# A decoder layer on one core: a second buffer and another order for the transposed probabilities of the cross attention

## The chip, the cores and the metric

The kernel runs on one core of a Trainium2 chip. The metric is the device time of one launch in microseconds; the lower the better. Five engines work beside each other: TensorE (PE), VectorE (DVE), ScalarE (ACT), GpSimd (POOL) and the DMA-issuing SyncE (SP). TensorE reads SBUF and writes PSUM, which has eight banks of 128 partitions by 512 fp32 values.

## What is computed

One pre-norm decoder layer on x of (8, 100, 512) with a context of (8, 361, 256), all fp32. Cut to its frame:

```python
x = x + attn(layernorm(x), ...)             # rope, 16 query heads on 4 key heads
x = x + xattn(layernorm(x), ctx_1024, ...)  # the part that the change touches
x = x + ffn(layernorm(x), ...)              # shared expert, and top 4 of 60 experts

# xattn, 16 heads of 32, 345 context rows and 16 more with weights of their own ("dca")
q = ln(x @ Wq + bq); k = ln(y_main @ Wk + bk); v = y_main @ Wv + bv
k_dca = ln(y_dca @ Wk_dca + ...); v_dca = ...
ctx = softmax(q @ k.T * SCALE) @ v + softmax(q @ k_dca.T * SCALE) @ v_dca
out = ctx @ Wo + bo
```

## The kernel before

**The whole.** One program with five hand-written instruction streams, one per engine, that meet at semaphores. After a preamble (weights, the dca keys) comes a loop over four pairs of batch rows; pair i holds batches 2i and 2i+1, called j = 0 and 1. Each turn does the self attention, the projections of the context, the cross attention, the output projection, the third layer norm and the router's gate. After the loop come the shared expert, the sorting of tokens to experts, the 60 experts in 20 rounds, and the gathering of the results. The change is in the cross attention of the loop alone.

**Steps.** The cross attention of a pair has 32 heads (two batches of 16), in 8 groups of four, `FOURS`. The TensorE stream walks `STEPS` = 10 steps, t = 0 to 9 (`for t in range(STEPS)`, line 1016 on). In step t it issues, in this order:

- `four_scores(t)` (L913), the scores of group t: four products of 32 rows by 345 columns, head r into bank r. It waits until ScalarE has emptied all four banks of the group before.
- `four_values(t - 2)` (L935): twelve products of 115 rows and 32 columns with the transposed probabilities of group t - 2. In steps 2 and 6, where a batch begins, a product with a tile of zeros (L930) first clears the whole bank (6 or 7), so that the others only add to it.
- `four_transposes(t - 1, c)` for c = 0 and 1 (L922): the probabilities of group t - 1, cut into three parts c of 115 rows; four transposes each.
- the work of `STEP_HOOKS`, that is other work hung on a step: a transpose of the queries in 3, dca scores in 4 (L883), dca transpose and the spread of the sums in 5 (L891, L947), the output projection of batch 0 in 6 (L787), dca transpose in 8. In step 5 `context_end(0)` (L900) follows behind everything.
- `four_transposes(t - 1, 2)`.

The parts c go to banks 4 and 5 by turns, so part 2 takes the bank of part 0 and can only begin when part 0 has been copied away.

**The other engines.** VectorE takes for each head the negated maximum (`four_max`, L1666), and copies the transposed parts from PSUM to `xpT` (`four_T`, L1670). Its stream also holds the layer norm of the next pair, cut into small linked pieces that `few(n)` drops between the others, n at a time. Its order in step t is

```python
four_max(t, 0); four_max(t, 1); few(1)
four_max(t, 2)
four_T(t - 1, 0)
four_max(t, 3)
few(2); four_T(t - 1, 1)
few(2); four_T(t - 1, 2)
few(2)
```

with `context_T(0)` behind the second maximum of step 6, and in step 7 `residual("xo", 0)` and the start of the third layer norm behind the fourth maximum. ScalarE takes the exponentials with their sums (`four_exp`, L1276), one for each head, into SBUF, and copies only the very last part 1 (L1325). There is one buffer `xpT` for the three parts of a group. `q_T(1)` (L1234) on ScalarE stands behind the exponentials of step 3; the scores of step 4 wait for it.

## Time and profile before

| | |
|---|---|
| median of 3 runs | 1371.33 us (1367.48 to 1371.35) |
| profiled execution, its own time | 1366.12 us |
| its span | 1364.3 us |
| busy shares of the span | PE 85%, PE weight load 45%, DVE 36%, POOL 29%, ACT 18% |
| mean granted clock of TensorE | 0.882 |
| chain that ended last | PE 48%, POOL 18%, DMA 11%, issue 11%, DVE 6% |

A busy time is what an engine's instructions take, without register, branch, semaphore and DMA-issuing ones. The profile marks for each stretch the granted clock of TensorE (PEclk): 1.00 is 2.4 GHz, 0.50 is 1.2 GHz, and a number between them means that part of the stretch had the one and part the other. Ends of matmuls are modelled, so the starts are what to compare. fp32 matmuls show as two records each, transposes as one.

### The profile page before, as it was taken

To read this page: it belongs to the slowest core of one execution; us is meant where nothing else is said; L and a number is where in the kernel's file an instruction comes from. 1 tells how busy PE (TensorE), PEld (TensorE's weight loads), DVE (VectorE), ACT (ScalarE), POOL (GpSimd) and SP (SyncE) were. 2 spreads that over 40 slices of the span, in tenths; PEclk is the share of its full clock that TensorE was granted. 3 is DMA by queue.
4 is the path that set the end of the run, shared out by engine and by line. 5 is a ranking of instruction groups with operands and counts; after the bars stand their busy time and mean duration, and the time that the engine had idled before them with its cause. 6 is when DMAs were issued, how large, how long until landed. Compare 5 with 4: busy or idle time off the path is not lost.

```text
span 1364.3 us, 18670 instructions
## 1 busy us (share of the span) xinstructions
PE 1165.7 (85%) x5358; PEld 617.7 (45%) x5358; DVE 493.3 (36%) x1360; ACT 251.2 (18%) x788; POOL 396.6 (29%) x917
## 2 busy tenths in 40 slices
PE   2988989888899899898879989999898989989920
PEld 0444564446544465444646544335444444444400
DVE  7342645337553474526644601002121212111224
ACT  0141321323231241413312000001010101111100
POOL 4686206852088403874000170000000000000045
PEclk8999679986899877997679998999898989999965
DMA  9997000000100001002027285008999999999835
GB/s 317 341 392 273 1 20 32 22 0 1 33 19 22 0 2 51 1 1 83 1 79 197 70 268 217 0 0 318 386 386 381 387 389 392 387 383 390 323 107 149
DMA packets 76438, 232.71 MB, mean 171 GB/s; under 512 B 11346, under 2 KB 13750, under 8 KB 68670
## 3 DMA queue, kind: packets, MB, share of 16 engines
q1 hardware_dynamic: 58686, 197.55, 40.0%
q10 hardware_dynamic: 11520, 20.98, 4.3%
q0 software_dynamic: 6144, 13.13, 3.3%
q8 instruction: 41, 0.67, 0.2%
q14 instruction: 47, 0.39, 0.1%
HBM read 178.40 MB, written 53.22 MB: 170 GB/s over the span
## 4 chain that ended last, share of the span: by engine, by line
PE 48%; POOL 18%; DMA 11%; issue 11%; DVE 6%; SPq 2%; POOLq 2%; ACT 1%; DVEq 0%; ACTq 0%
PE ps L1048 9%; DMA arena<-in_w 7%; PE ps L1125 6%; PE ps L1098 6%; PE ps L1121 5%; PE ps L787 4%; POOL arena L663 4%; PE ps L922 3%; PE ps L1156 3%; PE ps L1152 3%; DMA arena<-ys_d,slot_u 2%; PE ps L913 2%; POOL arena L660 2%; PE ps L935 2%; POOL arena L685 2%
## 5 line engine op out<-in xcount | busy, mean ns | idle before, releaser
L787 PE MATMUL ps<-arena 128*100 128x512 f32 (+3 forms) x576 | 233.8, 562 | 5.6 <-ACT arena L1223 3.7
L734 POOL DMA_INDIRECT arena<-ys_d,slot_u x32 | 34.6, 1082 | 503.1 <-issue 498.4
L787 PEld LDWEIGHTS ps<-arena 128*100 128x100 f32 (+1 forms) x576 | 95.1, 188 | 121.7 <-issue 111.5
L1125 PE MATMUL ps<-arena 128*64 128x352 f32 x640 | 115.4, 520 | 29.0 <-issue 17.0
L1048 PE MATMUL ps<-arena 128*128 128x400 f32 x352 | 126.4, 519 | 15.2 <-issue 8.3
L869 PE MATMUL ps<-arena 128*100 128x512 f32 x256 | 114.5, 592 | 0.0
L1874 DVE COPY arena<-ps 128x512 f32<-128x512 f32 x40 | 27.7, 692 | 229.0 <-PE ps L1113 229.0
L1048 PEld LDWEIGHTS ps<-arena 128*128 128x128 f32 x352 | 69.2, 198 | 71.0 <-issue 22.0
L1121 PE MATMUL ps<-arena 128*128 128x352 f32 x320 | 98.0, 459 | 1.2 <-DVE arena L1874 1.2
L1125 PEld LDWEIGHTS ps<-arena 128*64 128x64 f32 x640 | 53.5, 154 | 83.2 <-issue 63.4
L1276 ACT ACTIVATE arena<-ps,arena 100x345 f32<-100x345 f32 x128 | 69.1, 546 | 119.2 <-DVE arena L1666 118.7
L922 PE MATMUL ps<-ident,arena 100*115 100x100 f32 x384 | 75.2, 354 | 11.1 <-DVE arena L1670 11.1
L1098 PE MATMUL ps<-arena 128*100 128x512 f32 x176 | 75.8, 592 | 0.7 <-DVE arena L1853 0.7
L1368 ACT ACTIVATE arena<-ps 128x352 f32<-128x352 f32 x40 | 18.6, 465 | 312.9 <-PE ps L1121 168.8
L922 PEld LDWEIGHTS ps<-ident,arena 100*115 100x115 f32 x384 | 64.5, 254 | 24.1 <-DVE arena L1670 12.7
L1121 PEld LDWEIGHTS ps<-arena 128*128 128x128 f32 x320 | 59.2, 190 | 31.0 <-DVE arena L1868 1.4
L869 PEld LDWEIGHTS ps<-arena 128*100 128x100 f32 x256 | 42.0, 167 | 59.7 <-issue 57.3
L1666 DVE TENSOR_REDUCE arena<-ps 100x1 f32<-100x345 f32 x128 | 60.8, 508 | 20.3 <-PE ps L913 19.2
L1670 DVE COPY arena<-ps 115x400 f32<-115x400 f32 x92 | 52.6, 572 | 41.6 <-PE ps L922 41.5
L723 POOL DMA_INDIRECT xs_d<-arena,slot_u x32 | 31.9, 998 | 104.6 <-DVE ov_i L1841 95.1
L663 POOL TENSOR_TENSOR arena<-arena 115x256 f32<-115x256 f32 (+7 forms) x128 | 57.7, 451 | 10.0
L1156 PE MATMUL ps<-arena 128*64 128x512 f32 (+1 forms) x240 | 56.0, 601 | 0.7 <-DVE arena L1890 0.7
(209 smaller groups left out, 1456.6 us busy)
## 6 DMA issues: line engine op xcount, KB each, us to landing
arena<-in_w SPq DMA_DIRECT2D x60, 1408.0 KB, 12.6
arena<-in_w SPq DMA_DIRECT2D x60, 512.0 KB, 13.6
xs_d<-zero SPq DMA_DIRECT2D x5, 3328.0 KB, 26.0
arena<-in_w SPq DMA_DIRECT2D x60, 192.0 KB, 14.3
arena<-xs_d ACTq DMA_DIRECT2D x40, 256.0 KB, 8.0
ys_d<-arena ACTq DMA_DIRECT2D x40, 256.0 KB, 7.6
ys_d<-zero SPq DMA_DIRECT2D x2, 3328.0 KB, 24.8
arena<-in_se_up SPq DMA_DIRECT2D x11, 512.0 KB, 3.4
```

The lines of the kernel that those rows point to most:

```text
L663: then(nc.gpsimd.tensor_tensor(s3[:, :, 0:w], s3[:, :, 0:w], s3[:, :, w:2 * w], ALU.add))
L787: last = nc.tensor.matmul(ps[0:m, k, 0:cols[1] - cols[0]], lhs(c), w[:, c, cols[0]:cols[1]], start=(c == 0), stop=(c == n_c - 1))
L869: last = nc.tensor.matmul(ps[0:S, j, :], cT[c % 2][:, g, :], w_out[:, c * G + g, :], start=(c == 0 and g == 0), stop=(c == KV - 1 and g == ...
L922: last = nc.tensor.transpose(ps[0:LC, k, r * S:(r + 1) * S], xp[(4 * t + r) % NP_][0:S, c * LC:(c + 1) * LC], ident[0:S, 0:S])
L1048: last = nc.tensor.matmul(ps[:, (u % 3) * 2 + gu, 0:400].rearrange("p (a b) -> p a b", a=4), se_w[m % 3][:, c, gu * P:(gu + 1) * P], tok, ...
L1098: last = nc.tensor.matmul(ps[0:S, b % 4, :], hT_all[:, m, b * S:(b + 1) * S], w_down[:, m, :], start=(m == 0), stop=(m == MC - 1))
L1121: last = nc.tensor.matmul(ps[:, 1 + gu, 0:I], xsT[0][:, c, :], w13_s[s][0][:, c, at:at + I], start=(c == 0), stop=(c == DC - 1))
L1125: last = nc.tensor.matmul(ps[half * HALF:(half + 1) * HALF, 3 + gu, 0:I], xsT[1][:, c, half * HALF:(half + 1) * HALF], w13_s[s][1 + half][ ...
L1156: last = nc.tensor.matmul(ps[half * HALF:(half + 1) * HALF, 7, :], hT[1][0:w, n, half * HALF:(half + 1) * HALF], w2_s[s][1 + half][0:w, n, :],
L1276: nc.scalar.activation(xp[(4 * t + r) % NP_][0:S, :], ps[0:S, k, 0:LM], ACT.Exp, bias=xnm[0:S, j, h:h + 1], scale=1.0, accum_out=xsum[0:S, ...
L1666: nc.vector.tensor_reduce(xnm[0:S, j, h:h + 1], ps[0:S, k, 0:LM], AX, ALU.max, negate=True).then_inc(xmax_ready.sem, 1)
L1670: nc.vector.tensor_copy(xpT[0:LC, c, :], ps[0:LC, k, 0:4 * S]).then_inc(free[k].sem, 1)
```

## The change

Four edits go together:

1. `xpT` becomes two buffers, used by turns (t % 2). The second lies in SBUF space that held keys and values of the self attention (`behind_kr`).
2. In the TensorE stream the transposes of parts 0 and 1 stand straight behind the scores, and `four_values(t - 2)` behind them. The table of bank fills is changed to match. The zero product that begins a batch now reads all 128 rows of the zero tile instead of one; its columns are the same.
3. In the VectorE stream the four maxima of a step stand together, with `few(1)` after the second; the copies of parts 0 and 2 follow, each behind a `few(2)`. In step 6 `context_T(0)` goes behind the fourth maximum. In step 7 the residual and the start of the norm now stand ahead of both copies.
4. The copy of part 1 goes to ScalarE, behind the four exponentials of the step (in step 3 ahead of `q_T(1)`).

```diff
@@ attention_fills
         if t < FOURS:
             out += [(("xs", t, r), r) for r in range(4)]
+        parts = [(("xpT", t - 1, c), 4 + (t * LN_ + c) % 2) for c in range(LN_)] if 1 <= t <= FOURS else []
+        out += parts[:2]
         if t in (2, 6):
             out.append((("ctx", (t - 2) // 4), 6 + (t - 2) // 4))
-        parts = [(("xpT", t - 1, c), 4 + (t * LN_ + c) % 2) for c in range(LN_)] if 1 <= t <= FOURS else []
-        out += parts[:2] + [(key, 7 if t < 6 else 6) for key in STEP_HOOKS.get(t, [])] + parts[2:]
+        out += [(key, 7 if t < 6 else 6) for key in STEP_HOOKS.get(t, [])] + parts[2:]
@@ buffers
-        xpT = pT.rearrange("p a b c -> p (a b c)")[:, 0:LN_ * 4 * S].rearrange("p (a b) -> p a b", a=LN_)
+        behind_kr = arena[:, kr_at:kr_at + LN_ * 4 * S]
+        assert LN_ * 4 * S <= 3 * D
+        xpT = [v.rearrange("p (a b) -> p a b", a=LN_) for v in (pT.rearrange("p a b c -> p (a b c)")[:, 0:LN_ * 4 * S], behind_kr)]
@@ TensorE
-                        nc.tensor.matmul(ps[:, 6 + j, 0:DC * S], zero[0:1, 0:P], zero[0:1, 0:DC * S], start=True, stop=False)
+                        nc.tensor.matmul(ps[:, 6 + j, 0:DC * S], zero[:, 0:P], zero[:, 0:DC * S], start=True, stop=False)
...
-                    if t >= 2:
-                        four_values(t - 2)
                     if 1 <= t <= FOURS:
                         four_transposes(t - 1, 0)
                         four_transposes(t - 1, 1)
+                    if t >= 2:
+                        four_values(t - 2)
@@ ScalarE
+                def four_T(t):
+                    k = filled("xpT", t, 1)
+                    nc.scalar.activation(xpT[t % 2][0:LC, 1, :], ps[0:LC, k, 0:4 * S], ACT.Copy).then_inc(free[k].sem, 1)
...
+                    if t:
+                        four_T(t - 1)
                     if t == 3:
                         q_T(1)
@@ VectorE
                     four_max(t, 0)
                     four_max(t, 1)
+                    few(1 if t else 0)
+                    four_max(t, 2)
+                    four_max(t, 3)
                     if t == 6:
                         context_T(0)
-                    few(1 if t else 0)
-                    four_max(t, 2)
-                    if t:
-                        four_T(t - 1, 0)
-                    four_max(t, 3)
                     if t == 7:
                         residual("xo", 0)
                         run(pieces)
                         dve.wait_ge(x1_ready, i * 2 + 4)
                         pieces = norm_x(0)
                     if t:
-                        for c in (1, 2):
+                        for c in (0, 2):
                             few(2)
                             four_T(t - 1, c)
```

Two places of the order. Lines of the kernel before are 5 to 10 less than those of the same statement after. First VectorE, the second half of step 3, before; L1666 is a maximum, L1670 a copy of a transposed part, the rest are pieces of the norm:

```order
L1666 TENSOR_REDUCE arena<-ps 100x1
L403 REGISTER_ALU
L1670 COPY arena<-ps 115x400
L1666 TENSOR_REDUCE arena<-ps 100x1
L1434 REGISTER_ALU
L1477 TENSOR_SCALAR arena<-arena 100x1
L1434 REGISTER_ALU
L1453 TENSOR_SCALAR arena<-arena 100x1
L1454 TENSOR_SCALAR arena<-arena 100x1
L403 REGISTER_ALU
L1670 COPY arena<-ps 115x400
```

The same place in the change, where L1676 is the maximum and L1680 the copy:

```order
L1676 TENSOR_REDUCE arena<-ps 100x1 x2
L1444 REGISTER_ALU
L1487 TENSOR_SCALAR arena<-arena 100x1
L1444 REGISTER_ALU
L1463 TENSOR_SCALAR arena<-arena 100x1
L1464 TENSOR_SCALAR arena<-arena 100x1
L408 REGISTER_ALU
L1680 COPY arena<-ps 115x400
```

The first copy of the step, that of part 0, has moved from between the maxima to behind both of them and behind two pieces of the norm; one of three copies is gone.

Second TensorE, step 4, before (L913 scores, L935 values, L922 transposes, L883 dca scores):

```order
L913 MATMUL ps<-arena 100x345 x4
L935 MATMUL ps<-arena 32x100 x4
L409 REGISTER_ALU
...
L935 MATMUL ps<-arena 32x100 x4
L922 MATMUL ps<-ident,arena 115x100 x8
L880 REGISTER_ALU
L883 MATMUL ps<-arena 100x64 x4
L765 REGISTER_ALU
L922 MATMUL ps<-ident,arena 115x100 x4
```

And in the change (L918 scores, L927 transposes, L940 values, L888 dca scores):

```order
L918 MATMUL ps<-arena 100x345 x4
L770 REGISTER_ALU
L927 MATMUL ps<-ident,arena 115x100 x4
L770 REGISTER_ALU
L927 MATMUL ps<-ident,arena 115x100 x4
L940 MATMUL ps<-arena 32x100 x12
L885 REGISTER_ALU
L888 MATMUL ps<-arena 100x64 x4
L770 REGISTER_ALU
L927 MATMUL ps<-ident,arena 115x100 x4
```

The eight transposes have moved ahead of the twelve values, which now stand in one run; the last four transposes stay at the end of the step.

## Rows read from the trace of the kernel before

**Rows 1.** The granted clock of TensorE in 40 slices of the span.

```profile
PEclk8999679986899877997679998999898989999965
```

**Rows 2.** Busy times by stretch, pair 0, steps 2 to 7; the columns stand first.

```profile
core 0: us, PE busy (x) PEld busy (x) DVE busy (x) ACT busy (x) POOL busy (x), PEclk, DMA share, GB/s
148.55:155.01 6.46, 6.37 (x46) 4.26 (x47) 4.24 (x15) 2.34 (x8) 5.00 (x15) 0.53 0.02 4
155.01:161.40 6.39, 5.89 (x49) 4.39 (x49) 6.05 (x21) 2.92 (x9) 0.00 (x0) 0.50 0.00 1
161.40:167.88 6.48, 6.48 (x53) 5.02 (x53) 3.73 (x14) 2.34 (x8) 0.00 (x0) 0.50 0.01 3
167.88:176.43 8.55, 8.12 (x60) 6.36 (x59) 5.63 (x14) 3.07 (x10) 0.77 (x1) 0.50 0.00 0
176.43:186.42 9.99, 9.99 (x55) 5.57 (x54) 3.33 (x7) 2.65 (x9) 0.00 (x0) 0.67 0.01 2
186.42:196.58 10.16, 7.60 (x88) 5.82 (x87) 8.15 (x25) 3.07 (x10) 0.72 (x1) 0.84 0.01 2
```

**Rows 3.** The same of pair 1, steps 5 and 6, and of pair 2, step 3.

```profile
332.83:339.42 6.59, 6.16 (x60) 4.59 (x59) 5.64 (x14) 3.07 (x10) 0.79 (x1) 0.71 0.00 0
339.42:346.30 6.88, 6.88 (x55) 3.76 (x55) 3.33 (x7) 2.64 (x9) 0.00 (x0) 1.00 0.01 2
...
480.92:487.06 6.14, 4.60 (x49) 3.00 (x49) 5.93 (x22) 2.92 (x9) 0.00 (x0) 0.78 0.01 4
```

**Rows 4.** The same, cross attention of each pair, scores of step 0 to the gate.

```profile
136.02:201.02 65.00, 57.99 (x416) 38.81 (x417) 39.96 (x119) 22.77 (x74) 10.01 (x25) 0.64 0.01 2
301.33:360.58 59.25, 52.20 (x416) 34.66 (x417) 39.60 (x119) 22.78 (x74) 10.02 (x25) 0.70 0.01 2
462.88:521.19 58.31, 50.52 (x416) 33.31 (x417) 39.46 (x119) 22.77 (x74) 10.03 (x25) 0.73 0.01 2
624.24:689.34 65.10, 58.06 (x416) 38.78 (x417) 39.95 (x119) 22.78 (x74) 10.02 (x25) 0.63 0.05 19
```

**Rows 5.** Timeline of TensorE, pair 0, steps 1 and 2: start, length, work, [wait].

```profile
147.36 0.65 PE L922 MATMUL ps<-ident,arena 100*115 100x100 f32 x4 [2.21 <-DVE arena L1670]
148.55 1.19 PE L913 MATMUL ps<-arena 32*100 32x345 f32 x8 [0.54 <-ACT arena L1276]
149.44 1.54 PE L930 MATMUL ps<-zero 1*128 1x400 f32 x2
152.06 2.86 PE L922 MATMUL ps<-ident,arena 100*115 100x100 f32 x12
```

**Rows 6.** Timeline of VectorE, pair 0, step 1.

```profile
146.74 0.56 DVE L1670 COPY arena<-ps 115x400 f32<-115x400 f32 x1
```

**Rows 7.** Timeline of TensorE, pair 0, step 4.

```profile
161.40 1.49 PE L913 MATMUL ps<-arena 32*100 32x345 f32 x8 [0.49 <-ACT arena L1234]
162.81 1.23 PE L935 MATMUL ps<-arena 115*32 115x100 f32 x24
163.97 1.87 PE L922 MATMUL ps<-ident,arena 100*115 100x100 f32 x8
166.91 1.04 PE L922 MATMUL ps<-ident,arena 100*115 100x100 f32 x4
```

**Rows 8.** Timeline of VectorE, pair 0, step 4.

```profile
162.87 0.94 DVE L1666 TENSOR_REDUCE arena<-ps 100x1 f32<-100x345 f32 x2 [1.10 <-PE ps L913]
```

**Rows 9.** Timeline of TensorE, pair 0, steps 7 and 8.

```profile
186.42 0.84 PE L913 MATMUL ps<-arena 32*100 32x345 f32 x8
189.45 0.65 PE L922 MATMUL ps<-ident,arena 100*115 100x100 f32 x4 [0.56 <-DVE arena L1670]
191.99 0.38 PE L935 MATMUL ps<-arena 115*32 115x100 f32 x8 [1.59 <-DVE arena L1670]
```

**Rows 10.** Groups by line and form, pair 0, steps 1 to 6.

```profile
L1276 ACT ACTIVATE arena<-ps,arena 100x345 f32<-100x345 f32 x24 | 13.0, 545 | 26.0 <-DVE arena L1666 25.8
L1670 DVE COPY arena<-ps 115x400 f32<-115x400 f32 x17 | 9.7, 572 | 7.3 <-PE ps L922 7.3
```

More of the change, by code:

```diff
@@ L197, in decoder_kernel @@
         qr = [carve(D) for _ in range(2)]
+        kr_at = top[0]
         kr = [carve(KV, G, HD) for _ in range(2)]
@@ L935, in four_values @@
                             nc.tensor.matmul(ps[r * HD:(r + 1) * HD, 6 + j, a * S:(a + 1) * S], vx[j][0:LC, c, h * HD:(h + 1) * HD],
-                                             xpT[0:LC, c, r * S:(r + 1) * S], start=False, stop=False)
+                                             xpT[t % 2][0:LC, c, r * S:(r + 1) * S], start=False, stop=False)
                 def context_end(j):
@@ L1321, in _ @@
                             dca_exp(1)
+                    if t:
+                        four_T(t - 1)
                     if t == 3:
                         q_T(1)
-                k = filled("xpT", FOURS - 1, 1)
-                nc.scalar.activation(xpT[0:LC, 1, :], ps[0:LC, k, 0:4 * S], ACT.Copy).then_inc(free[k].sem, 1)
+                four_T(FOURS - 1)
                 dca_T(1)
@@ L1669, in four_T @@
                     k = filled("xpT", t, c)
-                    nc.vector.tensor_copy(xpT[0:LC, c, :], ps[0:LC, k, 0:4 * S]).then_inc(free[k].sem, 1)
+                    nc.vector.tensor_copy(xpT[t % 2][0:LC, c, :], ps[0:LC, k, 0:4 * S]).then_inc(free[k].sem, 1)
                 def context_T(j):
```

## Prediction

> **What bounds the kernel now.** I read the page first, then busy times by stretch, then the timelines of the bounding engines. The clock row [rows 1] shows TensorE short of full clock for much of the first half of the span, where the four pairs run. By pair [rows 4], the cross attention takes 65.00, 59.25, 58.31 and 65.10 us, 247.7 together, 18% of the span, at a mean granted clock of 0.63 to 0.73. TensorE is busy for 52 to 58 us of each; VectorE, with 39 to 40, has some 20 us free.
>
> By step of pair 0 [rows 2], the reader is to see two regimes. In steps 2 to 5 the clock stands at 0.50 to 0.53 and TensorE is busy nearly throughout: 6.37 of 6.46, 5.89 of 6.39, 6.48 of 6.48, 8.12 of 8.55 us. There TensorE at 1.2 GHz is the bound, and taking small waits away can win little. Where the clock is full, VectorE's order binds: in step 1 TensorE waits 2.21 us for a copy, then 0.54 for an exponential [rows 5], and in step 8 it waits 0.56 and 1.59 us for copies [rows 9]. What a higher clock is worth can be read by comparing pairs: steps 5 and 6 take 8.55 + 9.99 = 18.54 us in pair 0 at 0.50 and 0.67 [rows 2], and 6.59 + 6.88 = 13.47 in pair 1 at 0.71 and 1.00 [rows 3]. The work is the same; 5.07 us lie between.
>
> So the question is less which wait goes than whether the clock comes back sooner. In pair 0 it fell right behind the waits of step 1 (step 2 is at 0.53) and did not return through steps 3 to 5, though TensorE hardly rested. The Trainium skill (TensorE: Matmul & The Clock Gate, Part 1) says that the clock returns once the engine has been busy for a while and falls when it idles; this trace disagrees on the first half. What ran in those steps uses little of the array: scores of 32 rows, values of 32 columns.
>
> **The change part by part.** The sum is made for the profiled execution (1366.12 us; span 1364.3).
>
> *Second buffer.* It adds no instruction, and takes away only a limit that the old order never reached: 0. It makes edits 2 and 4 possible.
>
> *Copy of part 0 behind the fourth maximum.* In step 1 the copy began at 146.74 [rows 6]; now a maximum (half of 0.94 [rows 8]) and two small pieces, some 0.4, go ahead. The last four transposes come near 148.25 instead of 147.36 [rows 5]. They had 1.2 us before the next scores, which waited for exponentials; these come a copy's 0.5 earlier. The scores start at about 148.85 instead of 148.55: +0.3 a pair, **+1.2**. Bounds: 0, if the transposes still fit, and +0.9.
>
> *Copy of part 1 on ScalarE.* The nearest price is ScalarE's exponential of 345 columns, 545 ns [rows 10], against the copy's 572 on VectorE: 7 copies of 0.5 us a pair leave VectorE. They cost ScalarE nothing where it waits; it waited 25.8 us for maxima in steps 1 to 6 [rows 10]. The uncovered place is step 3, where the copy stands ahead of `q_T(1)`, for which the next scores wait [0.49 us, rows 7]. There the fourth exponential comes 0.5 us earlier and the copy takes it back: 0.
>
> *Step 3.* It gains hardly anything at any clock: the chain last maximum, exponential, `q_T(1)` ends it. In pair 2 it took 6.14 us at a clock of 0.78 [rows 3], in pair 0 6.39 at 0.50 [rows 2]. 0.1 a pair: **-0.4**.
>
> *Zero product with 128 rows.* Same columns, and it took 1.5 us for its two records at low clock [rows 5] with one row; length bounded by 0 and by that of a bigger one, still 1.5: 0. It lies in the middle of step 2, with clock at its lowest. For 1.5 us it uses the whole array. In pair 0 the clock came back in step 6 [rows 2], when full-size products (L787, 128 rows) ran; I take it that full-size zero rows act alike, and that in every pair the clock is full after step 2.
>
> *Steps 5 and 6 of pairs 0 and 3* (the two at 0.64 and 0.63 [rows 4]) then come down to pair 1's: 2 x 5.07 = **-10.1**. Pairs 1 and 2 have this already.
>
> *Step 4, all pairs.* At half clock it is TensorE throughout, 6.48 us. At full clock TensorE needs 3.2 of it, and VectorE's chain binds: scores 0.84 [rows 9], four maxima 1.9, three small pieces 0.5, copy 0.57, four transposes about 0.5: 4.3. Bounds: 0 and -2.2. I take -1.0, since the clock may have dipped in step 3, where TensorE idles before the copy: **-4**.
>
> *Step 5, all pairs.* Its maxima start earlier than pair 1's, by one copy (0.5) and by the maximum that no longer waits behind one. Bounds 0 and -2; taken -1.0: **-4**.
>
> *Clock falling again.* A faster TensorE waits more for VectorE, and in step 1 such waits came ahead of a fall. One relapse a pair in steps 4 to 6: step 6 at 0.67 costs 3.11 us more than at 1.00 [rows 2, 3]; half of this, 1.5, times four: **+6**. Bounds 0 and +12.
>
> *Steps 7 to 9.* The copy of part 0 in step 7 now stands behind the residual and the norm's statistics (operations of 512 columns, some 0.7 us each by the copy's 0.57 for 400) and a small piece, and behind the fourth maximum (0.5), so the 0.56 us wait grows to some 2.7; the wait of 1.59 inside the values goes, since both copies come close together. By hand the last values start 1.3 us earlier at full clock and 1.3 later at half: taken **0**, bounds -5 and +5.
>
> *Order on TensorE.* Values now stand between transposes, one more change of tile shape a step. In step 2 twelve transposes in a row took 2.86 us [rows 5]; in step 4 eight and four apart took 1.87 + 1.04 = 2.91 [rows 7]. So 0.05 a step, 28 steps: **+1**. The Trainium skill (TensorEngine Tiling (Array Packing), Key Properties) says that a change of tiling mode drains the engine; no separate drain shows in these rows, and by the page alone this order would cost more than the +1.
>
> Sum: 1.2 - 0.4 - 10.1 - 4 - 4 + 6 + 1 = -10.3, so 1355.8 for the profiled execution. The median of the runs is 5.2 above that execution; the forecast for the median is **1361**. Outside the cross attention nothing changes. The other runs differ by 4 us among themselves.
>
> **Rivals.**
>
> *A, the clock does not care* (0.25). A product of zeros with 128 rows may not count, or the low-use mix of step 3 keeps the clock down whatever step 2 did. For: steps 3 to 5 of pair 0 never recovered by themselves. Against: in pairs 1 and 2 it did recover in step 5, so the mix lies near the edge. Then steps 2 to 6 stay TensorE-bound at the old lengths, and what is left is +1.2 - 0.4 + 1 = +1.8: **1373**. The Trainium skill (same page as above, Part 4) says that transposes do not count as work for the full clock; by that rule the step, with twelve transposes in it, would stay low as here.
>
> *B, slower: the copy of part 0 comes too late* (0.12). Place: the last four transposes of a step, which wait for it, with the next scores queued behind. It decides once TensorE finishes values and hook before VectorE has passed the fourth maximum and two pieces; in steps 1 and 7 this is so in any case. Price a pair: 0.3 (step 1), 1.3 (steps 7 to 9), 1.7 for a relapse at a place now full (about half of 3.11): 3.3, times four +13: **1384**. Against: VectorE has 20 us of slack a pair.
>
> *C, the clock holds throughout* (0.13). Without the +6, and with -5 in steps 7 to 9: -21.3, **1350**; with steps 4 and 5 at their bounds 1341.
>
> **How the numbers follow.** The forecast has 0.50. Its own spread is about 7 us each way, from steps 4 and 5, the relapses and steps 7 to 9. A measurement can tell about 0.3%, 4.1 us. Faster than that: 0.85 of the forecast, all of C, a little of A: 0.59. Within: a seventh of the forecast and most of A: 0.25. Slower: B and a rest of A: 0.16. The range takes in the forecast, A, and C but for its far end, and leaves B out: 1344 to 1376.
>
> **What would show it.** In the changed profile, by stretch: step 3 at nearly full clock in every pair, its length still about 6 us; steps 5 and 6 of pairs 0 and 3 together near 13 us; step 4 near 5.5. TensorE's wait for a copy in step 1 at about 3 us. ScalarE's copies at 0.5 us, 7 a pair more. The forecast is wrong if the clock in steps 3 to 5 of pair 0 is still 0.50 (A), or if TensorE's waits for VectorE's copies grow by more than 3 us a pair and the clock falls where it was full (B).

## The result, and the profile after

The changed kernel is slower: 1372.91 us against 1362.94 for the kernel before (medians of 20 runs each; 1361.75 to 1394.4 and 1350.33 to 1385.77). The ratio is 1.0082, 95% interval 1.0054 to 1.011. Ratios here leave disturbed runs out, so they differ a little from the quotient of two medians. The forecast was 1361 and faster: 10.3 us below the kernel before, whose median then stood at 1371.33 (three runs). The change moved it 10 us the other way. The profiled execution took 1373.51 us (span 1371.7), 7.4 above that of the kernel before (1366.12).

The busy times by stretch, for the four pairs from the scores of step 0 to the gate, as in [rows 4].

```profile
135.04:199.89 64.85, 55.40 (x417) 36.29 (x417) 37.29 (x112) 24.95 (x81) 9.96 (x25) 0.68 0.00 1
304.19:367.18 62.99, 53.77 (x417) 35.39 (x417) 37.64 (x112) 24.95 (x81) 9.99 (x25) 0.71 0.00 1
470.77:532.63 61.86, 52.29 (x417) 34.33 (x417) 37.29 (x112) 24.95 (x81) 9.98 (x25) 0.72 0.00 1
635.36:700.25 64.89, 55.44 (x417) 36.08 (x417) 37.60 (x112) 24.95 (x81) 10.00 (x25) 0.69 0.05 19
```

The pairs take 254.6 us together, against 247.7 before: +6.9. Pairs 0 and 3 stayed at their 65 us, and pairs 1 and 2, which had been at 59.25 and 58.31, rose to 63 and 62. The loss lies in the loop: the shared expert behind it starts at 705.5 us instead of 697.4, and the part from the first expert's product to the last took 378 us against 379.

The same view by step, pair 0, steps 2 to 5, as in [rows 2]:

```profile
147.40:153.74 6.34, 6.34 (x47) 3.83 (x46) 4.85 (x13) 2.62 (x9) 4.50 (x13) 0.54 0.01 4
153.74:159.87 6.13, 3.61 (x49) 2.53 (x49) 5.37 (x19) 3.20 (x10) 0.00 (x0) 1.00 0.01 1
159.87:166.50 6.63, 6.63 (x53) 4.99 (x53) 2.88 (x11) 2.62 (x9) 0.00 (x0) 0.51 0.01 2
166.50:175.24 8.74, 8.31 (x60) 6.37 (x59) 5.15 (x13) 3.46 (x11) 0.77 (x1) 0.50 0.00 0
```

The reader is to see a clock (the third number from the end of a row) that comes and goes within two steps. Step 3 is at 1.00, as the forecast had it (before: 0.50), yet takes 6.13 us, and TensorE is busy for only 3.61 of them. Steps 4 and 5 are at half clock again. In pair 1 it is the same, and there a step is lost that had been fast before [rows 3]:

```profile
316.85:322.14 5.29, 5.29 (x47) 3.30 (x46) 4.69 (x13) 2.62 (x9) 4.27 (x15) 0.68 0.01 3
322.14:328.67 6.53, 4.01 (x50) 2.85 (x49) 5.52 (x18) 3.20 (x10) 0.58 (x1) 0.89 0.01 1
328.67:335.40 6.73, 6.73 (x52) 5.09 (x52) 3.24 (x13) 2.62 (x9) 0.00 (x0) 0.50 0.01 2
335.40:344.14 8.74, 8.31 (x59) 6.37 (x58) 5.15 (x13) 3.46 (x11) 0.79 (x1) 0.50 0.00 0
344.14:352.95 8.81, 8.81 (x56) 4.79 (x55) 2.75 (x6) 2.93 (x10) 0.00 (x0) 0.79 0.01 2
```

Steps 5 and 6 took 6.59 + 6.88 = 13.47 us in this pair before and take 8.74 + 8.81 = 17.55 now. Over the four pairs, steps 5 and 6 cost 7.7 us more, step 4 0.9, step 1 1.5, steps 7 and 8 with what follows to the gate 0.5; step 2 gives 3.6 back (it took 6.5 to 6.8 us, and takes 5.3 to 6.3, since the clock rises in it), steps 0 and 3 are as they were. Together +7.0, the +6.9 above.

What TensorE does in pair 0, steps 1 to 4, in its timeline:

```profile
146.37 1.09 PE L927 MATMUL ps<-ident,arena 100*115 100x100 f32 x4 [2.96 <-DVE arena L1680]
...
150.47 1.59 PE L935 MATMUL ps<-zero 128*128 128x400 f32 x2
151.99 1.23 PE L940 MATMUL ps<-arena 115*32 115x100 f32 x24
153.15 0.66 PE L927 MATMUL ps<-ident,arena 100*115 100x100 f32 x4
153.74 0.84 PE L918 MATMUL ps<-arena 32*100 32x345 f32 x8
...
158.41 0.65 PE L927 MATMUL ps<-ident,arena 100*115 100x100 f32 x4 [1.71 <-DVE arena L1680]
159.87 1.38 PE L918 MATMUL ps<-arena 32*100 32x345 f32 x8 [0.81 <-ACT arena L1239]
```

Behind the zero product the four transposes take 0.66 us instead of 1.04: the clock is full. Step 3 then waits 1.71 us for VectorE's copy and 0.81 for `q_T(1)` (2.10 and 0.42 in pair 1), and within the next scores the clock has fallen (1.38 us for eight records, against 0.84 just before at full clock). TensorE's waits for copies by VectorE come to 30.7 us in 15 waits over the whole span, all ahead of transposes (in all, times, longest; from the view of the waits):

```profile
PE ps L927 <- DVE arena L1680: 30.7, 15, 3.0
```

Before, there were two such rows, ahead of transposes and ahead of values, 19.1 us together:

```profile
PE ps L922 <- DVE arena L1670: 11.1, 8, 2.2
PE ps L935 <- DVE arena L1670: 8.0, 8, 1.6
```

So the waits grew by 11.6 us, 2.9 a pair. By step: step 1 waits 2.96 us a pair instead of 2.21; the waits of steps 7 and 8 come to 2.8 a pair instead of 2.6, in two places instead of three; step 3, which had no such wait, has 1.71 to 2.11.

### The profile page after: what moved, and what is told of

It reads as the page before. It is cut to its first block, busy times and chain, and to the rows that moved or that the text cites. A ratio compares the mean times of both kernels' runs of the same rounds, so it can differ in the third digit from the quotient of the medians.

```text
span 1371.7 us, 18670 instructions
## 1 busy us (share of the span) xinstructions
PE 1160.6 (85%) x5358; PEld 611.2 (45%) x5358; DVE 483.3 (35%) x1332; ACT 259.7 (19%) x816; POOL 397.1 (29%) x917
## 4 chain that ended last, share of the span: by engine, by line
PE 47%; POOL 19%; DMA 13%; issue 11%; DVE 5%; SPq 3%; POOLq 2%; ACT 1%; DVEq 0%; ACTq 0%
PE ps L1053 9%; DMA arena<-in_w 8%; PE ps L1130 6%; PE ps L1103 6%; PE ps L1126 5%; PE ps L792 4%; POOL arena L668 4%; PE ps L927 4%; PE ps L1161 3%; PE ps L1157 2%; POOL arena L665 2%; PE ps L918 2%; PE ps L940 2%; POOL arena L690 2%; DMA arena<-ys_d,slot_u 2%
## 5 line engine op out<-in xcount | busy, mean ns | idle before, releaser
L927 PE MATMUL ps<-ident,arena 100*115 100x100 f32 x384 | 73.8, 348 | 30.7 <-DVE arena L1680 30.7
L927 PEld LDWEIGHTS ps<-ident,arena 100*115 100x115 f32 x384 | 62.9, 248 | 58.4 <-DVE arena L1680 33.6
L1676 DVE TENSOR_REDUCE arena<-ps 100x1 f32<-100x345 f32 x128 | 58.2, 507 | 24.2 <-PE ps L918 23.2
L1680 DVE COPY arena<-ps 115x400 f32<-115x400 f32 x64 | 36.6, 572 | 55.3 <-PE ps L927 55.3
```

The lines of the kernel that those rows point to most:

```text
L927: last = nc.tensor.transpose(ps[0:LC, k, r * S:(r + 1) * S], xp[(4 * t + r) % NP_][0:S, c * LC:(c + 1) * LC], ident[0:S, 0:S])
L1676: nc.vector.tensor_reduce(xnm[0:S, j, h:h + 1], ps[0:S, k, 0:LM], AX, ALU.max, negate=True).then_inc(xmax_ready.sem, 1)
L1680: nc.vector.tensor_copy(xpT[t % 2][0:LC, c, :], ps[0:LC, k, 0:4 * S]).then_inc(free[k].sem, 1)
```

## The experiments

Two theories stood at the start. **T1** (theory 1): the copy of part 0, now behind four maxima, comes too late and starves TensorE. **T2** (theory 2): the order on TensorE (transposes ahead of values) costs time of its own and of the clock. **T3** came after the first four runs: the zero product of 128 rows costs time, and what it gives is lost in step 3. First each part of the change alone, in the whole kernel, in runs that share one base (before 1364.85 us, median of 23). All of them have the two buffers; the edits are shown shortened.

**Zero product alone** (`zero_only`).

```
-  nc.tensor.matmul(ps[:, 6 + j, 0:DC * S], zero[0:1, 0:P], zero[0:1, 0:DC * S], start=True, stop=False)
+  nc.tensor.matmul(ps[:, 6 + j, 0:DC * S], zero[:, 0:P], zero[:, 0:DC * S], start=True, stop=False)
```

> The kernel before with the zero product of 128 rows alone (and the unused second buffer). Theory 1 (the late copy of part 0 starves TensorE) and theory 2 (transposes ahead of the values cost TensorE time) both say that this part helps: in the changed profile the clock is full right behind it and step 2 takes 5.3 to 6.3 us where it took 6.5 to 6.8, so 2 to 5 us less in all; 0.9965 to 0.9985. If zeros don't count for the clock: 1.000, and step 2 as before.

Measured: 1371.43 us, ratio 1.0097 [1.0055, 1.0138]. Both theories missed: the product costs time where they foresaw a gain.

**Order on TensorE alone** (`pe_order_only`).

```
-  if t >= 2: four_values(t - 2)
   if 1 <= t <= FOURS:
       four_transposes(t - 1, 0)
       four_transposes(t - 1, 1)
+  if t >= 2: four_values(t - 2)
```

> The kernel before with the transposes of parts 0 and 1 ahead of the values, on TensorE alone (with two buffers). Theory 2: at half clock the changed profile's step 4 took 6.63 to 6.73 us against 6.48, with no wait in either: 0.15 to 0.25 us a step, 28 steps, 4 to 7 us more, 1.003 to 1.005. Theory 1: within 1 us, 1.000.

Measured: 1377.32 us, ratio 1.0119 [1.0034, 1.0205]: T2's direction, and more than its 1.003 to 1.005 at the middle of the interval.

**VectorE's order alone** (`dve_order_only`): four maxima first, then the copies, all on VectorE. `context_T(0)`, the residual and the norm stand as in the change.

```
   four_max(t, 0); four_max(t, 1); few(1 if t else 0)
-  four_max(t, 2); four_T(t - 1, 0); four_max(t, 3)
-  few(2); four_T(t - 1, 1)
+  four_max(t, 2); four_max(t, 3)
+  few(2); four_T(t - 1, 0); four_T(t - 1, 1)
   few(2); four_T(t - 1, 2)
```

> The kernel before with VectorE's four maxima ahead of all copies (three copies still on VectorE, residual and norm ahead of them in step 7). Theory 1: TensorE's wait in step 1 grows from 2.21 to about 3 us, in step 7 from 0.56 to over 2, and the clock falls sooner: 6 to 12 us more, 1.005 to 1.009. Theory 2: 1.000 to 1.002.

Measured: 1364.97 us, the median of before, with a ratio of 1.0064 [1.0022, 1.0107]. The ratio is what T1 expected; but the loss isn't in the loop, where T1 has its place: in the profiled execution the shared expert starts at 697.6 us (before 697.4, the change 705.5).

**Copy of part 1 on ScalarE alone** (`act_copy_only`): `four_T(t - 1)` on ScalarE behind the four exponentials, VectorE's order as before without that copy.

> The kernel before with the copy of part 1 on ScalarE alone. Theory 1: 0 to 3 us less, since VectorE has 7 copies a pair less, 0.998 to 1.000. Theory 2: the same. If the copy delays q_T(1) and the scores behind it: 1 to 2 us more, with a longer wait before the scores of step 4.

Measured: 1370.45 us, ratio 1.0127 [1.0053, 1.0201].

No part gains anything alone in the whole kernel. The whole kernel is a coarse scale: the experts' part behind the loop varies with its waits for weights, from 373 to 394 us in the profiled executions of these kernels. So most of the next kernels are cut behind the loop of pairs: they leave out the shared expert, routing and experts, and their output is what the loop leaves. Their times compare with each other, not with those of whole kernels.

**Cut kernels: before, the change, zero product alone, TensorE's order alone.** The edits are the ones above.

> The kernel before without everything behind the loop of pairs (shared expert, router, experts, gathering), whose DMA waits vary from run to run; the output is the sum behind the cross attention. It sets the base: about 700 us, by the profile of before, in which the shared expert starts at 697, with a spread of a few us from TensorE's clock alone.

> The changed kernel cut in the same way. All theories: 6 to 11 us above loop_before, since the full kernels differ by 10 at the median and the changed profile reaches the shared expert 8 us later. If the whole difference came from behind the loop: under 2 us.

> The cut kernel before with the 128-row zero product alone. Theory 3: at half clock the 128-row product no longer overlaps the tiles of its neighbours; scores to zero to values took 1.42 + 1.63 us in the run zero_only against 1.24 + 1.46 in before, 0.35 us at 8 places, 3 us more, and the clock that it wins in step 2 is lost in step 3, so +2 to +5 us. Theory 1 in its first form (the product helps): -2 to -5 us.

> The cut kernel before with the transposes ahead of the values alone. Theory 2: step 4 took 6.74 us in the run pe_order_only against 6.48, step 2 7.03 against 6.81, step 5 8.74 against 8.55: 0.2 to 0.25 us a step, 28 steps, +5 to +7 us, and more where the clock comes back later. Theory 1: within 1 us.

Measured: before 716.11 us (708.61 to 729.6), the change 724.94 (716.25 to 728.99), zero product 722.06 (720.53 to 724.34), order 736.85 (732.81 to 739.07), six runs each. By the medians the change costs the loop 8.8 us, near the 8.1 by which its shared expert starts later; but the runs of the two kernels overlap, so the size is not sharp. The order alone costs 20.7, clear of the spread. The spread comes from the clock: the four pairs of the kernel before, 65.0, 59.3, 58.3 and 65.1 us in the whole kernel, are 57.9, 58.3, 65.0 and 59.8 in its cut one, with the same code. Which pairs get the clock back early changes from one execution to the next. With the change they are 61.9 to 65.1 in both.

The parts do not add up: something in the change gives back what the order costs. Pair 1 with the order alone, steps 4 and 6:

```profile
327.49:334.22 6.73, 6.73 (x52) 5.10 (x52) 3.73 (x14) 2.34 (x8) 0.00 (x0) 0.50 0.01 2
...
342.96:355.40 12.44, 12.44 (x56) 6.01 (x55) 3.23 (x7) 2.64 (x9) 0.00 (x0) 0.56 0.00 1
```

The order itself costs 0.25 us in step 4 (6.73 against 6.48, both at 0.50 and without a wait), 0.2 in steps 2 and 5 (7.03 against 6.81, 8.74 against 8.55). The rest is the clock: in all four pairs it stays at 0.50 until the projection of step 6 (11.2 to 12.6 us; it took 6.88 to 10.04 in the cut kernel before).

**The change without TensorE's order; VectorE's order alone; ScalarE's copy alone**, all cut.

> The whole change but for the order on TensorE (values stay ahead of the transposes), cut behind the loop of pairs like the other cut kernels (before cut: 716.1 us, change cut: 724.9, order alone: 736.9). Theory T2 (what the change loses is the order on TensorE: two more changes of tile shape a step, and a clock that comes back later): 703 to 716 us, no slower than before cut. Theory T1 (the loss is the copy of part 0 that comes behind the fourth maximum): stays within 4 us of the change, 721 to 729. Theory T3 (the zero product of 128 rows): 718 to 724, since it is still in.

> Before, cut, with nothing but VectorE's order changed (four maxima ahead of the copies of parts 0 and 1, transposed probabilities in two buffers). T1: slower than before cut by 4 us or more, 720 or above, with TensorE's waits for a copy in steps 1 and 7 longer. T2: 710 to 718, since maxima that end earlier start the exponentials earlier and the waits that grow lie in three places a pair only.

> Before, cut, with nothing but the copy of part 1 moved to ScalarE. T1: within 3 us of before cut (713 to 719), since the copy of part 0 does not move. T2: 708 to 716, since it leaves VectorE 0.57 us a step free, and any gain shows where the clock is full (steps 1, 6, 7).

Measured: 723.95 us (720.89 to 725.38), 713.04 (707.1 to 726.82) and 721.14 (715.64 to 729.74). T1 falls: VectorE's order, with the late copy of part 0, costs the loop nothing alone, and beside the zero product it and ScalarE's copy add 1.9 us (722.06 to 723.95). T2 falls as the reason for the whole: without the new order the change has about the same time, 1.0 us less by the medians. T3 fits. Both theories missed on ScalarE's copy, for which neither foresaw a loss; its +5 is within the spread of the cut kernels, but in the whole kernel the interval lies above 1. In the cut kernel's profile step 3 takes 6.8 us in every pair (6.3 to 6.9 in the whole one; before 6.1 to 6.5), as it would with the copy standing ahead of `q_T(1)`; that this is the reason was not tested.

**The change with the one-row zero product**, cut (the zero product's edit taken back).

> The change, cut behind the loop, with the zero product back at one row. Alone, TensorE's new order cost 20.7 us (736.9 against 716.1), but with the rest of the change about 1 (724.9 against 724.0 without it). If the zero product of 128 rows is what gives those 20 us back (it lifts the clock in steps 2 and 6), this run comes to 733 to 742. If VectorE's order and the copy on ScalarE give them back, it comes to 714 to 725.

Measured: 734.57 us (731.66 to 735.5). So the zero product gives back what the order costs: with the order, going to 128 rows brings 9.6 us (734.6 to 724.9, and the runs do not overlap); without it, it costs 6 (716.1 to 722.1; this lies within the spread of the cut kernel before, but the whole kernel's ratio of 1.0097 is clear of 1). Two parts of the change depend on each other, and neither pays against the old order.

Why does it cost alone? TensorE's timeline of step 2, at half clock, in the cut kernel before and then with the zero product:

```profile
305.36 1.49 PE L841 MATMUL ps<-arena 32*100 32x345 f32 x8 [0.28 <-ACT arena L1066]
306.60 1.54 PE L858 MATMUL ps<-zero 1*128 1x400 f32 x2
308.06 1.23 PE L863 MATMUL ps<-arena 115*32 115x100 f32 x24
```

```profile
145.16 1.49 PE L845 MATMUL ps<-arena 32*100 32x345 f32 x8
146.58 1.70 PE L862 MATMUL ps<-zero 128*128 128x400 f32 x2
148.22 1.23 PE L867 MATMUL ps<-arena 115*32 115x100 f32 x24
```

From scores to values 2.70 us lie with one row and 3.06 with 128: 0.36 us more, up to twice a pair, at half clock. The one-row product starts 1.24 us behind the scores' start, the full one 1.42 behind it. And step 5, which in the cut kernel before was at 0.72 to 0.84 in three of four pairs, is at 0.50 in all four (8.55 us). In pair 2 the product does not bring the clock back at all (steps 2 and 3 at 0.50, in 7.16 and 6.48 us). In the others step 3, at 0.82 to 0.94, ends in waits as in the change (1.50 us for a copy and 0.98 for `q_T(1)` in pair 1), and step 4 is at 0.50.

**Filling the waits.** If a clock that has come back is lost in the waits of steps 1 and 3, products of zero placed in those waits should keep it. They add zero to the sum of heads, which is open then (bank 6 or 7); its first product moves from step 2 to step 1. The cut kernel before, with two such products in step 1, two ahead of the last transposes of step 3 and two ahead of the values of step 8:

```
+  def warm(j, n, first=False):
+      for k in range(n):
+          nc.tensor.matmul(ps[:, 6 + j, 0:DC * S], zero[:, 0:P], zero[:, 0:DC * S], start=(first and k == 0), stop=False)
...
+  if t == 8: warm(1, 2)
   if t >= 2: four_values(t - 2)
   if 1 <= t <= FOURS: four_transposes(t - 1, 0); four_transposes(t - 1, 1)
+  if t == 1: begin("ctx", 0); warm(0, 2, first=True)
   for key in STEP_HOOKS.get(t, []): hooks[key[0]](*key[1:])
+  if t == 3: warm(0, 2)
   if 1 <= t <= FOURS: four_transposes(t - 1, 2)
```

> Before, cut, but with products of zero put where TensorE waits: the sum of heads is begun in step 1 with two 128-row zero products in the 2.2 us wait, two more stand ahead of the last transposes of step 3 and two ahead of the values of step 8. If the clock falls because of the waits (what T1 and T2 both take), it stays up behind step 1 in some pairs and the time is 695 to 712. If the small-tile work of steps 2 to 5 itself takes the clock down whatever goes before, the added products cost about 0.2 to 0.4 us each: 717 to 724.

Measured: 691.7 us (689.48 to 704.61), 24.4 below the cut kernel before and below the range expected. Steps 1, 2 and 4 are at 1.00 in all four pairs; step 3 loses the clock at a wait of 1.04 us ahead of the values' last part, and its two fillers then run at half clock for 2.9 us in pair 1.

**Fillers in step 1 alone**, cut.

> Before, cut, with the fillers of step 1 alone: the sum of heads begun there with two zero products of 128 rows in TensorE's wait of 2.2 us; nothing in steps 3 and 8. If the wait of step 1 is what takes the clock away in step 2, step 2 runs at 0.9 to 1.0 in 4.2 to 4.6 us in every pair and the whole is 700 to 710, short of 691.7 since step 8 still has its waits. If all fillers are needed: 712 or more.

Measured: 715.35 us (712.53 to 719.45): the step came as expected and the sum didn't. Pair 1, steps 2 and 3:

```profile
311.66:315.91 4.25, 3.12 (x45) 2.16 (x45) 4.15 (x16) 2.34 (x8) 3.19 (x14) 1.00 0.02 4
315.91:323.51 7.60, 5.34 (x48) 3.85 (x49) 7.39 (x22) 2.92 (x9) 1.81 (x2) 0.67 0.00 1
```

Step 2 falls from 6.81 to 4.25 us, and step 1 keeps its 5.21. But step 3 rises to 7.6 us, bound by VectorE (busy 7.39 of 7.60), and hands step 4 a half clock (6.48 us at 0.50). That is the same trade as in the changed kernel: a gain in step 2, a fall in step 3. Not all of step 2's gain is the clock: the first zero product has left it for a wait, which is worth some 0.8 us a pair (an estimate, from the 0.86 us that such a product takes in step 6 at full clock).

**Whole kernels with fillers in every wait.** First the kernel before (two products in step 1, one ahead of the values' last part in step 3, two ahead of `spread_T(0)` in step 5, two ahead of the values of step 8); then the changed kernel (three in step 1, two ahead of the last transposes of step 3, two in step 5, three ahead of the last transposes of step 7):

```
   if 1 <= t <= FOURS: four_transposes(t - 1, 0); four_transposes(t - 1, 1)
+  if t == 1: begin("ctx", 0); warm(0, 3, first=True)
   if t >= 2: four_values(t - 2)
   for key in STEP_HOOKS.get(t, []):
+      if key == ("rx", 0): warm(0, 2)
       hooks[key[0]](*key[1:])
+  if t == 3: warm(0, 2)
+  if t == 7: warm(1, 3)
   if 1 <= t <= FOURS: four_transposes(t - 1, 2)
```

> The whole kernel before, with fillers where TensorE waits: two zero products of 128 rows in step 1, one ahead of the last part of the values in step 3 (wait 1.04 us in the run with fillers; the two ahead of that step's last transposes, which ran at half clock for 2.9 us, are gone), two ahead of the transposes of the gates in step 5 (wait 1.46), two ahead of the values in step 8. If waits of TensorE are what takes the clock away, steps 2 to 5 stay at 0.9 to 1.0, step 3 falls from 8.6 to about 6 us, step 6 from 9.8 to 7, and the whole is 1325 to 1342 (before: 1363 to 1365). If the small-tile work itself takes it away in step 3: 1338 to 1350. If the gain of the loop is lost behind it: 1355 or more.

> The whole changed kernel with fillers where it waits: three zero products in step 1 (wait 2.96), two ahead of the last transposes in step 3 (1.71), two ahead of the gates' transposes in step 5, three ahead of the last transposes in step 7 (2.62). If the change lost by its longer waits and the clock that they cost, it comes within 5 us of the old kernel with fillers. If its order on TensorE costs time of its own at full clock too, it stays 6 us or more behind that one.

Measured, against a base of 1354.26 us (1338.83 to 1367.06) in these runs: 1325.33 us (1321.66 to 1338.5), ratio 0.9812 [0.9747, 0.9876], and **1307.1 us** (1304.61 to 1308.87), ratio **0.9661 [0.9614, 0.9707]**. The changed kernel with fillers beats both kernels, and the kernel before with fillers by 18, where it was expected within 5 of it or behind. Its pair 1, steps 1 to 6, and 7 and 8 together:

```profile
297.97:303.32 5.35, 4.43 (x28) 2.61 (x27) 4.70 (x15) 2.73 (x9) 3.63 (x9) 1.00 0.00 0
303.32:307.53 4.21, 3.04 (x45) 2.12 (x44) 3.63 (x13) 2.63 (x9) 3.19 (x14) 1.00 0.02 4
307.53:314.37 6.84, 4.99 (x54) 3.16 (x53) 6.08 (x19) 3.20 (x10) 1.72 (x2) 1.00 0.00 1
314.37:318.45 4.08, 3.89 (x52) 2.90 (x52) 2.84 (x11) 2.62 (x9) 0.00 (x0) 1.00 0.02 4
318.45:324.73 6.28, 6.02 (x63) 4.17 (x63) 5.15 (x13) 3.12 (x11) 0.79 (x1) 1.00 0.00 0
324.73:331.97 7.24, 7.14 (x56) 3.69 (x55) 2.75 (x6) 3.17 (x11) 0.00 (x0) 1.00 0.01 2
331.97:344.43 12.46, 10.67 (x129) 7.43 (x129) 9.70 (x32) 4.48 (x13) 0.72 (x1) 1.00 0.01 3
```

From step 1 to the gate the clock is full in all four pairs, and each takes 53.7 to 53.8 us where the changed kernel took 61.9 to 64.9. Steps 5 and 6 are 6.28 + 7.24 = 13.5 us, step 4 4.1. The old kernel with fillers stays behind in step 3 (7.60 us at 0.91 in pair 1, VectorE busy 7.39) and in step 4 behind it (6.49 us at 0.50):

```profile
311.21:318.81 7.60, 4.54 (x50) 2.75 (x51) 7.39 (x22) 2.92 (x9) 1.81 (x2) 0.91 0.00 1
```

The fillers themselves, in the changed kernel's step 1, and the transposes behind them:

```profile
299.62 2.20 PE L932 MATMUL ps<-zero 128*128 128x400 f32 x6
302.74 0.65 PE L927 MATMUL ps<-ident,arena 100*115 100x100 f32 x4 [0.92 <-DVE arena L1695]
```

Waits of 0.9 to 1.2 us are still there (0.92 in step 1, 1.17 in step 2, 1.00 in step 3), and the clock held through them.

A filler does two things at once: it shortens a wait, and it is full-size work. No run here tells the two apart. That a full clock can last without any filler is shown by VectorE's order alone, cut, in pair 3, where steps 4 to 6 are at 1.00 with a wait of 1.46 us in step 5. Its steps 3 and 4:

```profile
643.40:649.23 5.83, 5.04 (x49) 3.42 (x49) 5.58 (x18) 2.80 (x9) 0.00 (x0) 0.70 0.02 4
649.23:653.32 4.09, 3.72 (x52) 2.83 (x52) 3.52 (x14) 2.23 (x8) 0.00 (x0) 1.00 0.01 4
```

**The same with values ahead of transposes**, and **the same with three more products ahead of step 0** (two between `begin("xqT", 0)` and its wait, one between `begin("ds", 0)` and its wait), where TensorE waits 1.89 and 0.78 us and step 0 is at 0.59:

> The changed kernel with the same fillers as the run before (1307.1 us, clock full from step 1 to step 8), but for the order on TensorE: values ahead of the transposes, as in the kernel before. Where the clock is held, the new order's own cost is small (about 0.25 us a step at half clock, so 0.1 at full) and its benefit is that the copies of a step start 0.7 us earlier. If that benefit is real, this run is 3 to 15 us slower, 1310 to 1322; if the order only ever cost, it is 1300 to 1306.

> The changed kernel with fillers, and three more products of zero a pair ahead of step 0, where TensorE waits 1.89 and 0.78 us and the clock then falls to 0.59 for step 0 (7.3 us, eight full-size products in it). If waits take the clock there too, step 0 falls to 5.2 to 5.6 us in all four pairs and the whole to 1297 to 1303. If something else takes it: 1306 to 1312.

Measured, against a base of 1362.11 us (1349.46 to 1376.31): 1322.05 us (1313.83 to 1325.88), ratio 0.9704 [0.9652, 0.9756], and 1316.51 (1313.42 to 1326.24), ratio 0.9688 [0.9636, 0.9739]. The base has moved by 8 us since the last runs, and by the ratios the three kernels lie within each other's intervals. The first, 15 us above 1307.1, looks like the 3 to 15 us expected for the order, but isn't: its steps 1 to 8 are equal to those of the changed kernel with fillers within 0.1 us (5.35, 4.19, 6.79, 4.09, 6.28, 7.24 and 12.46 us in pair 1), and its shared expert starts at 656.5 us, against 656.8. So where the clock is held the order on TensorE costs nothing and brings nothing. The difference lies behind the loop: in the up-projections of the shared expert TensorE stands 9.8 us in six waits that no engine ends, and the clock falls (0.87 over the stretch), where the other kernel runs through. The last stretch of those products, in this kernel and then in the changed kernel with fillers:

```profile
765.00:803.20 38.20, 27.70 (x74) 14.39 (x72) 3.41 (x6) 3.02 (x6) 10.47 (x11) 0.87 0.76 265
```

```profile
765.00:790.70 25.70, 25.00 (x75) 13.85 (x73) 2.85 (x5) 2.52 (x5) 10.75 (x11) 1.00 0.86 343
```

From the first of these products to the experts' first it takes 224.3 us here, 224.2 in the kernel before, 225.4 in the changed one, and 211.3 in the changed one with fillers; the kernel before with fillers has no such waits either (211.5). Those 13 us are in the 1307 and the 1325 and are no work of the fillers as such. The 40.6 us of the loop (697.4 to 656.8) are the work of the fillers with the change: 32.6 in the four cross attentions, the rest between them.

With fillers ahead of step 0 that step takes 4.42 us at 1.00 in every pair, from 7.3 at 0.59, and the shared expert starts at 649.6, 7.2 earlier. The whole missed its range all the same. More was there to be had: in pairs 2 and 3 the clock fell in step 4, behind a step 3 that looks the same as in pairs 0 and 1. Pair 2, steps 3 and 4:

```profile
447.62:454.42 6.80, 4.98 (x54) 3.16 (x53) 6.04 (x19) 3.20 (x10) 1.71 (x2) 1.00 0.00 1
454.42:459.81 5.39, 5.39 (x52) 4.25 (x52) 2.88 (x11) 2.62 (x9) 0.00 (x0) 0.64 0.01 3
```

Step 3 has its fillers and the same remaining waits (1.00 and 0.81 us), and the clock falls all the same: with the waits filled it fell in two of the twelve pairs of these three kernels. The kernel has the slow 225 us behind the loop too, so its total is not lower than 1307. Whether both gains can be had in one program was not tried.

## Why the prediction was wrong

By its own steps:

- **"I take it that full-size zero rows act alike, and that in every pair the clock is full after step 2"**, the step that failed. Its first half held: step 3 is at 1.00, 0.89, 0.98 and 0.90 in the four pairs. The second half was used for steps 4, 5 and 6, and there it doesn't hold: TensorE at full clock reaches step 3's copy and `q_T(1)` early, waits 1.71 and 0.81 us (pair 0), and steps 4 and 5 are at 0.50 in every pair. The step rested on one return of the clock, in step 6 of pair 0, and on full-size products as its reason; in pairs 1 and 2 it had come back with none running. The text had seen this danger ("the clock may have dipped in step 3") and priced it at a part of step 4's gain, with one relapse a pair at half its price. It was a full relapse in all four pairs.
- **Steps 5 and 6 of pairs 0 and 3, -10.1; step 5, -4; step 4, -4; relapse, +6**: together -12.1 forecast, +8.6 measured (7.7 for steps 5 and 6, 0.9 for step 4). Pairs 1 and 2 lost the recovery in step 5 which they had; only rival B priced such a loss, at 1.7 a pair. That pairs 0 and 3 were the slow ones was chance of that execution, as the cut kernel before shows. What the steps take at full clock was read rightly: 4.3 us was worked out for step 4 and 4.08 measured with fillers, 13.47 taken for steps 5 and 6 and 13.5 measured.
- **Order on TensorE, +1**: mis-sized. The rows it used, twelve transposes in a row against eight and four, had no change from transposes to values in them. At half clock the order costs 0.2 to 0.25 us a step, some 0.7 a pair in steps 2, 4 and 5, and alone it makes the clock return only in step 6: 20.7 us in the loop. At full clock it costs 0. The Trainium skill (TensorEngine Tiling (Array Packing), Key Properties) says that a change of tiling mode drains the engine, which the text set aside for want of a row; the 6.73 against 6.48 us of step 4 agree with it.
- **Zero product, 0**: mis-sized. It is 0.36 us each at half clock: the full-size product starts 1.42 us behind the scores, the one-row product 1.24.
- **Copy on ScalarE, 0**: in the change step 3 keeps its length, as worked out. Alone it makes step 3 some 0.4 us longer in each pair of the cut kernel.
- **Copy of part 0 behind the fourth maximum, +1.2**: right. The wait is 2.96 us ("about 3") and step 1 costs 1.5 over the pairs. Step 3, -0.4: it came to 0, at full clock and near 6 us as said. Steps 7 to 9, 0: it came to +0.5, the first wait 2.62 us ("some 2.7").

The measured 1372.9 is the number of rival A (1373), but not its mechanism, since the clock did care. Rival B's sign was right and its test was half met: the clock fell where it had been full (step 6 of pairs 1 and 2), but the waits for VectorE's copies grew by 2.9 us a pair, just under its 3. Its cause is not borne out: VectorE's late copy alone costs the loop nothing. The late copy lengthened step 1's wait (2.21 to 2.96 us, with the clock at 0.86 to 1.00 in both); step 3's new wait stands where TensorE became faster. The Trainium skill (TensorE: Matmul & The Clock Gate, Part 1) says that idling takes the clock away; here the runs with fillers agree, though not without exception. Its other half, that being busy brings it back, holds here in places only: in steps 2 to 5 of pair 0 before, 26.9 of 27.9 us busy [rows 2] did not bring it back, and in pairs 1 and 2 it came back inside step 5.

## What to carry to other kernels

Where a clock is short, ask of each stretch at full clock what ends it, not only what starts it: a faster engine reaches its waits sooner, and a stretch bound by another engine (here step 3) can hand a low clock to the next. Put harmless full-size products into such waits, measured to fit them, and only then judge the other edits: the same change that cost 10 us here is part of a version that is 47 us faster (some 13 of it from elsewhere). Test parts in pairs as well as alone, because the zero product cost 6 us without the new order and brought 10 with it. And look at more than one execution before calling one pair fast and another slow.

## What the runs showed of the hardware that was not expected

- The same small-tile work runs at either clock. Step 4 ran at 1.00 with TensorE busy 3.89 of 4.08 us, and at 0.50 with 6.73 of 6.73. Step 2 held 1.00 through a wait of 1.17 us while busy 3.04 of 4.21.
- The clock can come back in the middle of such work, with no full-size product running. In the kernel before, pair 2, the first eight transposes of step 5 begin at half clock, at which they take 1.87 us (1.05 at full clock), and the next two are at full clock; ahead of them stood scores, values, transposes and the dca scores. In step 3 of that pair it came back too [rows 3]. What decides between this and pair 0, where it stayed away, is not shown:

```profile
496.11 1.49 PE L922 MATMUL ps<-ident,arena 100*115 100x100 f32 x8
497.44 0.33 PE L891 MATMUL ps<-ident,arena 100*128 100x100 f32 x2
```

- At half clock a one-row product starts 1.24 us behind the start of the scores (32-row tiles), a 128-row one 1.42.
- With TensorE fast, step 3 begins while GpSimd still works on 512 columns, and two small VectorE operations on 100x1 take 0.90 and 1.01 us instead of 0.15. Each ends as GpSimd's operation ends (316.68 against 316.66 us, 317.73 against 317.72), and the copy behind them is late by some 1.6 us (0.90 + 1.01 less twice 0.15). The Trainium skill (SBUF — State Buffer, SBUF: two separate sides) says that VectorE's operations with two inputs from SBUF and GpSimd's hold one shared port pair by turns, the loser waiting the whole instruction out; the rows agree. The timelines of VectorE and GpSimd in the cut kernel with fillers in step 1, pair 1:

```profile
315.78 0.90 DVE L1183 TENSOR_TENSOR arena<-arena 100x1 f32<-100x1 f32 x1
316.72 1.01 DVE L1186 TENSOR_TENSOR arena<-arena 100x1 f32<-100x1 f32 x1
317.65 0.56 DVE L1395 COPY arena<-ps 115x400 f32<-115x400 f32 x1
```

```profile
315.62 1.04 POOL L629 TENSOR_TENSOR arena<-arena 100x512 f32<-100x512 f32 x1
316.63 1.09 POOL L644 TENSOR_TENSOR arena<-arena 100x512 f32<-100x512 f32 x1
```

- TensorE's six waits in the shared expert's up-projections (8.3 to 10.0 us, 13 with the clock) are there or absent with the same code in that part: absent in the two kernels with fillers of the first pair of runs, there in the others, one profiled execution each. What decides it stays open, and so does the fall of the clock in step 4 of the last run.
